# Barriers between the four stages of a fused attention and expert kernel: semaphores alone, GpSimd not drained

## What is computed

```python
x = x + _L0_xattn_ref(_layernorm(x), ctx_1024, ctx_1024, 16)        # 16 heads, rotary, ALiBi bias
x = x + _L0_ffn_ref(_layernorm(x), rms_w, gate_w, W1, b1, W2, b2)   # top-1 of 8 experts, silu
x = x + _L1_xattn_ref(_layernorm(x), ctx_1024, ctx_1024, Wq, bq, Wk, bk, Wv, bv, Wo, bo)
x = x + _L1_ffn_ref(_layernorm(x), gate_w, w1, w2)                  # each expert takes its 128 best tokens of a sequence, gelu
```

## Time and profile before

| | us |
|---|---|
| median of three runs | 1024.86 |
| the profiled execution, its own time | 1026.07 |
| its span, first to last instruction | 1024.3 |
| PE busy in it | 908.5 |
| DVE busy | 652.7 |
| ACT busy | 545.1 |
| POOL busy | 335.4 |

### The profile page before, as it was taken

The page is one execution under the profiler, slowest core; times in us unless marked ns, Lnnn a source line. Parts: engine busy times, 40 slices in busy tenths (PEclk is TensorE's granted clock), DMA queues, the critical chain, the costliest instruction groups (busy, mean ns, idle before and its releaser), DMA issues. The chain is left out here.

```text
span 1024.3 us, 17731 instructions
## 1 busy us (share of the span) xinstructions
PE 908.5 (89%) x6882; PEld 628.5 (61%) x6882; DVE 652.7 (64%) x1137; ACT 545.1 (53%) x796; POOL 335.4 (33%) x324
## 2 busy tenths in 40 slices
PE   4389999999789999999779988999896999799994
PEld 3133444444649999998624444444455888699994
DVE  7578989897341111111897867888584848877783
ACT  1147877777043232322527866767571555467771
POOL 7696763000012222223123023001002426467532
PEclk9559999999699999999959999999998989899997
DMA  7879474401479999994847183330023636558874
GB/s 256 177 217 201 115 180 90 71 5 65 157 264 404 375 345 347 330 331 151 187 111 150 31 156 117 79 71 4 22 85 98 211 102 174 168 178 253 256 225 106
DMA packets 57366, 175.77 MB, mean 172 GB/s; under 512 B 8496, under 2 KB 30640, under 8 KB 44560
## 3 DMA queue, kind: packets, MB, share of 16 engines
q1 hardware_dynamic: 40784, 138.74, 45.1%
q0 software_dynamic: 13296, 29.63, 10.9%
q10 hardware_dynamic: 3216, 6.43, 1.7%
HBM read 132.96 MB, written 40.76 MB: 170 GB/s over the span
## 5 line engine op out<-in xcount | busy, mean ns | idle before, releaser
L1096 DVE TENSOR_REDUCE a_row_max<-ps_ring 128x2 f32<-128x1024 f32 x256 | 308.2, 1222 | 69.0 <-PE ps_ring L828 67.7
L986 ACT ACTIVATE a_probs<-ps_ring 128x1024 f32<-128x1024 f32 x256 | 261.4, 1024 | 100.5 <-PE ps_ring L843 98.4
L862 PE MATMUL ps_out<-a_probs,a_vaug 128*32 128x256 f32 x2048 | 166.1, 397 | 2.0 <-ACT a_out_sb L992 1.3
L828 PE MATMUL ps_ring<-a_ka,a_qa 52*128 52x512 f32 (+1 forms) x512 | 124.3, 488 | 31.0 <-DMA a_ka<-scratch_k_scr 19.8
L843 PE MATMUL ps_ring<-a_qa,a_ka 56*128 56x512 f32 (+1 forms) x512 | 131.2, 509 | 4.0 <-DVE a_row_max L1096 3.4
L1394 ACT ACTIVATE e_hid<-ps_ring,e_wts 128x128 f32<-128x128 f32 x184 | 52.1, 371 | 115.3 <-DMA e_wts<-in_w 61.8
L843 PEld LDWEIGHTS ps_ring<-a_qa,a_ka 56*128 56x128 f32 (+1 forms) x512 | 48.9, 187 | 96.0 <-issue 66.3
L828 PEld LDWEIGHTS ps_ring<-a_ka,a_qa 52*128 52x128 f32 (+1 forms) x512 | 52.8, 204 | 66.0 <-ACT a_probs L986 21.9
L862 PEld LDWEIGHTS ps_out<-a_probs,a_vaug 128*32 128x32 f32 x2048 | 40.9, 108 | 78.3 <-issue 74.0
L1705 POOL DMA_INDIRECT scratch_acc<-e_ys,token x32 | 68.9, 2154 | 58.3 <-DVE e_ys L1849 37.9
L1482 PEld LDWEIGHTS ps_ring<-e_xst,e_wts 128*128 128x128 f32 x736 | 85.7, 192 | 2.0 <-issue 0.8
(11 more groups left out here) (293 smaller groups left out, 1371.7 us busy)
## 6 DMA issues: line engine op xcount, KB each, us to landing
a_probs<-in_w SPq DMA_DIRECT2D x32, 1024.0 KB, 5.3
e_wts<-in_w SPq DMA_DIRECT2D x23, 1156.0 KB, 8.8
e_wts<-in_w SPq DMA_DIRECT2D x23, 1024.0 KB, 8.2
a_qa<-scratch_q_scr SPq DMA_DIRECT2D x28, 384.0 KB, 9.0
a_ka<-scratch_k_scr SPq DMA_DIRECT2D x28, 384.0 KB, 7.0
scratch_q_scr<-a_qst POOLq DMA_DIRECT2D x36, 256.0 KB, 3.6
scratch_k_scr<-a_kst POOLq DMA_DIRECT2D x9, 512.0 KB, 8.3
scratch_q_scr<-a_qst SPq DMA_DIRECT2D x12, 256.0 KB, 3.3
```

Of the source, the lines that this page charges most:

```text
L828: ins = pe.matmul(to[:, par], qa[rows, b % 2, g, p, qt * P:(qt + 1) * P], ka[rows, b % 2, g, p], start=True, stop=True)
L862: ins = pe.matmul(m.ps_out[VW * h:VW * (h + 1), cols], vaug[:, b % NV, kc, HG * g + h], probs[:, t % 3, h, cols], start=(kc == 0 and half ...
L986: nc.scalar.activation(probs[:, t % 3, 2 * half:2 * half + 2], unit("s", n), ACT.Exp, scale=HD ** -0.5).then_inc(exp_done, 1)
L1096: dve.tensor_reduce(row_max[:, s % 3, qt, :, p], unit("m", n), AX.X, ALU.max).then_inc(mx_read, 1)
```

## The change

All three `with nc.Block()` get the option `no_gpsimd_drain=True`. [...] Since the attention function runs twice, four barriers change: three between stages and the one at the end. The barrier at the head of the program (L2041) stays. No instruction of a stage moves.

```diff
@@ -462,7 +462,7 @@
-        with nc.Block() as block:
+        with nc.Block(no_gpsimd_drain=True) as block:
```

## The result

| | before | after |
|---|---|---|
| median of 18 runs each, us | 1028.43 (1023.3 to 1041.51) | 1020.92 (1015.17 to 1032.32) |
| profiled execution's own time, us | 1026.07 | 1020.86 |
| its span, us | 1024.3 | 1018.9 |

The ratio is 0.992, with a 95% interval of 0.990 to 0.994: the changed kernel is 8.2 us faster (6.2 to 10.3). One slow execution of each kernel, 1041.51 and 1032.32 us, is left out of the ratio; the medians of all 18 lie 7.5 us apart. All engines carry out the same instructions in the same order in both kernels, but for the barriers.

What follows compares the result with a forecast made beforehand. At the three inner barriers all engines were taken to stand still for POOL's drain alone. Gains of 1.6 + 1.9 + 5.4 - 0.1 = 8.8 us from the 1024.86 us median gave 1016.1 us, range 1014 to 1018, wider 1012.5 to 1021.

Steps and rivals of the forecast that it cites:

- The three terms: Gains at the three inner barriers from releasing at the last other engine's arrival instead of POOL's drain end: 1.6, 1.9, 5.4 us.
- The third term: Barrier after the third stage: release moves from POOL's drain end, 783.96, to DVE's arrival, 778.53; 5.4 us.
- The first two: Barriers after the first and second stage: release goes with DVE's, then PE's arrival; 1.6 and 1.9 us.
- POOL never last: Third barrier: POOL's semaphore instruction passes its waiting gathers, so DVE sets the release; upper gain, 5.4 us.
- POOL arrives behind its own work: Rival: at the third barrier POOL's semaphore instruction waits until the gathers are issued; gain there 3.0 us, 1018.5 us total; chance 0.2.
- What is late next: Start of the fourth stage: DVE's path to the split (782.2) and the gather's landing path (782.0) tie, hiding the gather.
- The drains at the head: Rows cited from the program's head: with nothing behind them, ACT's drain took 8 ns and POOL's 169.
- The covered time: Rival: engines need the barrier pause anyway, above all for loading instructions; gain 0 to 4.5 us, 1022.5 us; chance 0.15.
- The clock: Rival: PE's clock adds gains behind the first and third barriers, up to 15 us in all; 1013 us likelier; chance 0.1.
- Room for descriptors: Slower rival: without drains POOL's descriptor list fills and its DMAs wait, 34 us over the second stage's tiles; 1050 us; chance 0.05.
- the wider one: Range 1012.5 to 1021 us, holding the forecast and first rival with parts of the clock and covered-time cases; 0.2 left out.

Runs made afterwards that it cites:

- the early drains: Kernel before with all its drains, plus one more POOL drain in its idle time of each of the first three stages; 1025.75 us, ratio 0.9953.
- Its harder form: Changed kernel with POOL waiting for its four gathers' landing before the third barrier; 1028.31 us, ratio 0.9997, and on a second run 1025.59 us, ratio 0.996.
- the second drain of a pair: Kernel before with six more POOL drains, two in a row at the end of each of the first two stages; run once, 1024.24 us.

## Why the prediction was right

**The barriers' sums.** The three terms were 1.6, 1.9 and 5.4 us, less 0.1. The waits fell by 1.75 - 0.15 = 1.60, by 2.02 - 0.23 = 1.79 and by 5.57 - 0.17 = 5.40: 8.8 together. The runs give 8.2 (6.2 to 10.3), and 11.1 (7.2 to 14.9) when repeated. Comparing the end of POOL's drain with the last other arrival was the right reading. The third term was borne out by itself (5.3 us for 5.5 us of waits). The first two came out with the early drains, together with 1.0 us of the third (4.8 us for 4.6), but not with their drains left out alone, for the reason given there. That both intervals for the whole change, from 6.2 and from 7.2 us, lie above 5.5 is what speaks for them in the changed kernel.

**The choice at the third barrier.** I took "POOL never last" from the semaphore wait that had passed waiting gathers. It holds: POOL arrives and is released while two gathers are still to end. The rival "POOL arrives behind its own work" is false, and would have had the release at 780.8 instead of 778.5. Its harder form, built as an experiment, costs 4.4 us of wait.

**What is late next.** Forecast were 778.8 for DVE's first operation, 782.2 for the split, 782.0 for ACT's end, with the gather's landing just hidden; measured 778.69, 782.10 and 781.91. PE's first transpose came at 780.17, against rows there at 780.3.

**The drains at the head.** This trace has drains near 10 ns where an engine has nothing to wait for: ACT's 8 ns at the head and SP's 7 at the second barrier; POOL's at the head took 169. The inner barriers' drains are not of that kind: PE's took 2.2 us and DVE's 0.45 behind their own work, and POOL's 3.8 us with nothing at work at all; the second drain of a pair took 53 and 34 ns.

**The other rivals.** The covered time is false: each stage's first operation follows the release by 0.2 to 0.4 us, as before. The clock added next to nothing. The changed kernel's windows right behind the first and the third barrier, columns as above:

```profile
259.80:264.80 5.00, 4.77 (x27) 4.80 (x27) 4.37 (x23) 0.31 (x1) 0.00 (x0) 0.61 0.65 212
782.90:786.90 4.00, 3.96 (x20) 3.99 (x21) 2.09 (x1) 1.33 (x3) 2.61 (x2) 0.54 0.55 137
```

The same stretches before (262.2 to 267.2 and 788.4 to 792.4) have 0.51 and 0.63: a little up at the one, a little down at the other. The 48 gate products, from the timeline, took 9.59 us for 10.38:

```profile
260.03 9.59 PE L145 MATMUL ps_out<-gate,xnt 128*128 128x8 f32 x48 [1.75 <-PEq L465]
```

That is 0.8 us, of the 4.7 that the rival had there at most, and the fourth stage took no less than before. The clock had not quite fallen yet at the release: it was 0.75 on average from 259.8 to 262.0 us, and 0.50 from there until the products ended. Before, the 2.2 us from 262.2 us, behind the release there, had 0.52. So it stayed up for a moment longer behind the shorter pause, and while the narrow products ran it did not come back, as the prediction had it. Room for descriptors is false as a mishap: the page's row for the second stage's scatters is nearly the same as before (121.6 us idle for 122.5), 987 ns each; and the fourth stage's 32 scatters (L1705), behind the 119 DMAs of the first three stages with no inner drain, took 2160 ns each for 2154. The second stage's row:

```profile
L1341 POOL DMA_INDIRECT scratch_ys<-e_ys,e_to_row x23 | 22.7, 987 | 121.6 <-DVE e_ys L1572 121.6
```

Yet it had the right thing in sight: something does pile up with POOL's DMAs, at 83 to 96 ns each and bounded, only that a later DMA doesn't pay for it; a later drain does. The prediction priced the drains' tails as they stood (3.7, 3.8, 3.0) and never asked what they were made of. Here that changed no number, because all drains that counted went at once.

**The level.** Forecast 1016.1, measured 1020.92. That lies outside the forecast's own range of 1014 to 1018, just inside the wider one (to 1021), and above the 1019.7 that was to count as faster. So the gain was right by its mechanism, but that the time itself fell inside the wider range was narrow, and in part luck. The step that is off is the start, not the change: the median before was 1024.86 in the three runs shown and 1028.43 in 18, so 3.6 of the 4.8 us are the baseline's; by the sum, 1028.43 - 8.8 = 1019.6. The rest, 1.3 us, is less than the spread of the runs, and no run tells what it is.

## What to carry to other kernels

At a barrier, set the end of each engine's drain beside the last other arrival; the difference, and not the drain's length, is what a change there can bring, and then look for what the next stage waits for in its place. POOL's drain here cost 83 to 96 ns for every DMA that POOL had issued since its last one up to 70 of them, and 6.57 us behind 115, so leaving some of the drains out brought nothing while a later one stayed on the path (1030.47 us, ratio 1.0014): leave out all that count, or put an extra one early, into POOL's idle time. And measure the baseline as often as the changed kernel before naming an absolute time: a difference was known to 2 us here, the level was not.

## What the hardware showed that I had not expected

- POOL's drain takes 83 ns for each of its DMAs since the last drain in two stages (45, 46) and 96 in a third (24), although all have landed; behind 70 it took 6.07 us and behind 115 only 6.57. The next drain takes 34 to 53 ns.
- POOL's semaphore instructions pass its pending gathers: it arrived at 778.4 us with two gathers still to run, until 780.80.
- The same stage of the same kernel took 299.3 and 304.8 us on two profiles, and behind its first softmax the clock stayed at 0.50 for 5.0 us more in one execution of the kernel before and for 14.6 us more in one of the changed kernel; and in one kernel it fell to 0.51 while PE was busy for 11.70 of 12 us.
